# Choice of experts split into single operations, logits in four blocks, the last logits kept on chip, w1 loaded early, five idle TensorE products

## What is computed

```python
def _L0_conv_ref(x, ...):          # attention over all tokens of an image, after a group norm
    h = group_norm(x, gn_scale, gn_bias, 16)
    q, k, v = nin(h, wq, bq), nin(h, wk, bk), nin(h, wv, bv)
    w = softmax(q @ k^T * C ** -0.5)
    return x + nin(w @ v, wo, bo)

t = t + _L1_attn_ref(_ln_t(t), Wq, Wk, Wv)      # causal attention, after a LayerNorm

def _L1_ffn_ref(x, gate_w, gate_b, weight1, weight2):     # x = _ln_t(t); 32 experts
    logits = einsum('bsd,ed->bse', x, gate_w) + gate_b
    probs = softmax(logits, axis=1)                        # over the tokens
    topv, topi = top 8 tokens of each expert
    pooled = einsum('bked,bke->bed', x[topi], topv)
    out = gelu(pooled @ weight1) @ weight2                 # with bias rows
    outputs[topi] += out * topv
t = t + outputs
```

## Time and profile before

| | us |
|---|---|
| median of 3 runs | 900.59 (899.41 to 900.7) |
| the profiled execution | 901.2 |
| its span in the profile | 899.4 |
| busy: PE / DVE / ACT / POOL | 803.9 / 566.2 / 506.4 / 371.0 |

### The profile page before, as it was taken

How to read it: one execution, slowest core, us unless ns; L and a number is a source line. 1 busy time by engine, 2 the same in 40 slices (tenths; PEclk the granted TensorE clock), 3 DMA queues, 4 the chain that set the end, 5 groups by cost and what they waited for, 6 DMA issues and landing times. The chain is left out here.

```text
span 899.4 us, 14859 instructions
## 1 busy us (share of the span) xinstructions
PE 803.9 (89%) x4406; PEld 473.2 (53%) x4406; DVE 566.2 (63%) x1493; ACT 506.4 (56%) x1096; POOL 371.0 (41%) x288
## 2 busy tenths in 40 slices
PE   4586999999999999999999999999999997755286
PEld 2253556565656565656565656565656553433155
DVE  3427476767676767676767676767777755451224
ACT  3153567676767666666676666666666663533120
POOL 3062536363636364545454545455454543100000
PEclk9997899999999999999999999999999998958558
DMA  1000000000000000000000000000000020010798
GB/s 46 0 1 12 1 13 25 18 24 19 24 19 24 19 24 18 24 18 24 18 24 18 24 18 24 18 24 18 24 18 24 7 71 30 1 31 1 147 239 230
DMA packets 62997, 30.54 MB, mean 34 GB/s; under 512 B 35279, under 2 KB 60271, under 8 KB 62959
## 3 DMA queue, kind: packets, MB, share of 16 engines
q1 hardware_dynamic: 62959, 30.05, 13.5%
HBM read 15.23 MB, written 10.49 MB: 29 GB/s over the span
## 5 line engine op out<-in xcount | busy, mean ns | idle before, releaser
L1025 DVE TENSOR_REDUCE neg_max<-maxima_in 128x1 f32<-128x1024 f32 (+7 forms) x256 | 252.0, 984 | 94.3 <-PE maxima_in L654 90.8
L862 ACT ACTIVATE probs<-scores 128x512 f32<-128x512 f32 (+3 forms) x464 | 233.0, 541 | 118.0 <-PE scores L681 106.4
L934 POOL TENSOR_TENSOR prob_sum<-prob_sum,probs 128x1024 f32<-128x1024 f32 x96 | 228.2, 2377 | 8.8 <-ACT probs L862 0.6
L654 PE MATMUL maxima_in<-keys,queries 128*128 128x512 f32 (+3 forms) x496 | 172.6, 422 | 17.3 <-DVE neg_max L1025 14.4
L681 PE MATMUL scores<-queries,keys 128*128 128x512 f32 (+3 forms) x464 | 173.0, 373 | 0.0
L654 PEld LDWEIGHTS maxima_in<-keys,queries 128*128 128x128 f32 x496 | 85.9, 200 | 89.9 <-DVE neg_max L1025 57.4
L696 PE MATMUL values_out<-probs,x_sb 128*64 128x512 f32 x512 | 129.4, 612 | 0.0
L908 POOL TENSOR_TENSOR ln<-ln_mv,eps_ln 128x8 f32<-128x8 f32 x32 | 6.5, 203 | 297.8 <-DVE ln_mv L1059 297.8
L679 PE MATMUL scores<-queries_lo,keys_hi 65*128 65x512 f32 x256 | 109.8, 429 | 2.2 <-DMA queries_lo<-max_rows 1.2
L681 PEld LDWEIGHTS scores<-queries,keys 128*128 128x128 f32 x464 | 90.5, 195 | 8.2
L696 PE MATMUL values_out<-probs,normed 128*64 128x128 f32 (+3 forms) x480 | 84.5, 441 | 0.1
(11 more groups left out here) (169 smaller groups left out, 1102.7 us busy)
## 6 DMA issues: line engine op xcount, KB each, us to landing
x_sb<-in_x SPq DMA_DIRECT2D x16, 256.0 KB, 2.9
u_all<-u_sb SPq DMA_DIRECT2D x16, 256.0 KB, 2.5
t_scratch<-t SPq DMA_DIRECT2D x16, 256.0 KB, 2.9
total<-t_scratch SPq DMA_DIRECT2D x16, 256.0 KB, 4.8
w_sb<-in_w SPq DMA_DIRECT2D x1, 2080.0 KB
logits_scratch<-logits SPq DMA_DIRECT2D x32, 64.0 KB, 2.1
lg<-logits_scratch SPq DMA_DIRECT2D x4, 512.0 KB, 3.7
out<-total SPq DMA_DIRECT2D x16, 128.0 KB, 2.2
```

The lines of the kernel that those rows point to most:

```text
L654: mm = pe.matmul(maxima_in[:, lo:lo + w * P], weights, keys[s][q][:, h * HALF:h * HALF + w * P], start=not diagonal, stop=True, skip_group ...
L862: nc.scalar.activation(of(probs[:, t % NP, :]), shape(scores[:, bank_of(s, u), 0:w]), ACT.Exp, scale=SCALE).then_inc(exp_done, 1)
L934: nc.gpsimd.tensor_tensor(prob_sum[:, :], before, probs[:, t % NP, :], ALU.add).then_inc(rows_added, 1)
L1025: V.tensor_reduce(neg_max[s][:, at:at + 1], maxima_in[:, HALF - widths[0] * P:HALF + widths[1] * P], AX.X, ALU.max, negate=True).then_inc( ...
```

## The change

- e.top becomes three steps, e.max, e.rep and e.ne. A table EXPERT_SLOTS says which step runs in which slot, for each engine apart, and the groups have a semaphore each (expert_step0 to 3). In turn 15 VectorE has one step in a slot, and TensorE's transposes start in slot 5.
- mlg makes the logits of an image in two products of 256 columns into 128 partitions of fin_ps, lg is one copy of 128 x 256, and sl has four stores of 32 partitions, where it had two of 64. gate_b_sb has 128 rows, filled by four loads.
- The last image: its products go to partitions 96 to 127 of two banks, from the halves of ut apart (64 rows each), and ScalarE writes them with the bias straight into the tile lg. SyncE loads the other three images of that group right after the last store of u.
- w1 lies over the keys and queries of the first attention. ScalarE issues its load in turn 15 after the last exponential of the first attention.
- expert_part: three products of 512 columns that nobody reads ahead of the last choice, one ahead of the turn by image, one ahead of the sums.
- In ScalarE's list lg comes ahead of its slot 0, and l1n ahead of its slots 5 and 6. Neither changes anything while the slots are empty.

```diff
+EXPERT_SLOTS = {
+    "dve": {0: [("e.max", 0)], 1: [("e.rep", 0)], 2: [("e.ne", 0)], 3: [("e.gate", 0)], 4: [("e.max", 1)], 5: [("e.rep", 1)],
...
-    if n == B:
-        return [(EXPERT_STEPS[k % 7], k // 7) for k in (2 * c, 2 * c + 1) if k < 14]
-    if n == B + 1 and c < 7:
-        return [(EXPERT_STEPS[c], 2)]
-    return []
+    return EXPERT_SLOTS[engine].get(c + NT * (n - B), [])
...
-                   (gate_b_sb[0:E, :], g["gate_b"]), (gate_b_sb[E:2 * E, :], g["gate_b"])]
+                   *[(gate_b_sb[r * E:(r + 1) * E, :], g["gate_b"]) for r in range(P // E)]]
...
+                if n.trip is None and n.first == B - 1:
+                    load_logits(NG - 1, BG - 1)
+            elif name == "sl" and (n.trip is not None or n.first < B - 1):
...
-                dst = image_of(logits_dram, at).rearrange("e (j a t) -> a e j t", a=2, t=P)
-                for a in range(2):
-                    sp.dma_start(dst[a], logits[a * E:(a + 1) * E, :].rearrange("e (j t) -> e j t", t=P)).then_inc(
-                        logits_stored, 16)
+                dst = image_of(logits_dram, at).rearrange("e (h j a t) -> h a e j t", h=2, a=2, t=P)
+                for h, a in itertools.product(range(2), range(2)):
+                    r = (2 * h + a) * E
+                    sp.dma_start(dst[h, a], logits[r:r + E, :].rearrange("e (j t) -> e j t", t=P)).then_inc(logits_stored, 16)
...
+            elif name == "mlg" and n.trip is None and n.first == B - 1:
+
+                pe.wait_ge(proj_step, done("proj_step", "yb", n, "lo"))
+                for a, bank in enumerate((fin_ps, proj_ps)):
+                    r = slice(a * C, (a + 1) * C)
+                    mm = pe.matmul(bank[P - E:P, :], gate_bd[r, a * E:(a + 1) * E], ut[r, :], start=True, stop=True)
+                mm.then_inc(fin_step, 1)
...
-                pe.matmul(fin_ps[0:2 * E, :], gate_bd[:, :], ut[:, :], start=True, stop=True).then_inc(fin_step, 1)
+                for h in range(2):
+                    mm = pe.matmul(fin_ps[h * 2 * E:(h + 1) * 2 * E, 0:HALF // 2], gate_bd[:, :],
+                                   ut[:, h * HALF // 2:(h + 1) * HALF // 2], start=True, stop=True)
+                mm.then_inc(fin_step, 1)
...
+            elif name == "lg" and n.trip is None and n.first == B - 1:
+                act.wait_ge(fin_step, done("fin_step", "mlg", n, "mm"))
+                act.wait_ge(g["expert_step"][NG - 3], done(f"expert_step{NG - 3}", "e.ne", NG - 3, "chosen"))
+                for a, bank in enumerate((fin_ps, proj_ps)):
+                    ins = nc.scalar.activation(
+                        g["lg"][P - E:P, (NG - 1) % 2, :].rearrange("p (j a t) -> p a j t", a=2, t=P)[:, a, :, :],
+                        bank[P - E:P, :].rearrange("p (j t) -> p j t", t=P), ACT.Identity, bias=gate_b_sb[P - E:P, :], scale=1.0)
+                ins.then_inc(fin_step, 1)
...
+            if s == 1 and u == len(UNITS[1]) - 1 and n.trip is None and n.first == B - 1:
+
+                nc.scalar.dma_start(g["w1_sb"][:, :, :], g["w1"].rearrange("e d h -> d e h")).then_inc(g["w1_loaded"], 16)
...
-        k = LAST_GROUP
-        sp.dma_start(g["lg"][:, k % 2, :], logits_dram[k * BG:(k + 1) * BG].rearrange("b e s -> (b e) s")).then_inc(
-            g["logits_loaded"][k], 16)
-        sp.dma_start(w1_sb[:, :, :], g["w1"].rearrange("e d h -> d e h")).then_inc(w1_loaded, 16)
...
+        def keep_clock(times, bank):
+
+            for _ in range(times):
+                pe.matmul(hidden_ps[:, bank, :], ident_f[:, :], g["u_all"][:, 0, 0:HALF], start=True, stop=True)
+
+        keep_clock(3, BANKS - 1)
...
         mm.then_inc(out_ready, 1)
+        keep_clock(1, 0)
         pe.wait_ge(out_biased, 1)
...
         mm.then_inc(image_turned, 1)
+        keep_clock(1, 0)
         pe.wait_ge(image_copied, 2)
```

More of the change, by code:

```diff
@@ L237, in choose_on_vector @@
 def choose_on_vector(nc, g, name, k):
-    V, step, lg, rest, top, stat, gates = (nc.vector, *(g[n] for n in ("expert_step", "lg", "rest", "top", "stat", "gates")))
+    V, lg, rest, top, stat, gates = (nc.vector, *(g[n] for n in ("lg", "rest", "top", "stat", "gates")))
+    step = g["expert_step"][k]
     def after(step_name):
-        before = done("expert_step", name, k, step_name, back=1)
+        before = done(f"expert_step{k}", name, k, step_name, back=1)
         if before > 0:
             V.wait_ge(step, before)
-    if name == "e.top":
-        after("max")
+    if name == "e.max":
         V.wait_ge(g["logits_loaded"][k], 16)
@@ L251, in choose_on_vector @@
         V.tensor_scalar(stat[:, k, 0:1], top[:, k, 0:1], -1.0, None, ALU.mult).then_inc(step, 1)
+    elif name == "e.rep":
+        if k > 0:
+            V.wait_ge(g["expert_step"][k - 1], done(f"expert_step{k - 1}", "e.gate", k - 1, "gates"))
+        after("rest")
         V.match_replace(rest[:, :], top[:, k, :], lg[:, k % 2, :], NEG_HUGE).then_inc(step, 1)
+    elif name == "e.ne":
         after("chosen")
@@ L263, in choose_on_scalar @@
 def choose_on_scalar(nc, g, name, k, turn, pool_ps):
-    step, gates, gates_t, pool_sb, pooled = (g[n] for n in ("expert_step", "gates", "gates_t", "pool_sb", "pooled"))
+    gates, gates_t, pool_sb, pooled = (g[n] for n in ("gates", "gates_t", "pool_sb", "pooled"))
+    step = g["expert_step"][k]
     if name == "e.exp":
-        nc.scalar.wait_ge(step, done("expert_step", "e.top", k, "neg"))
+        nc.scalar.wait_ge(step, done(f"expert_step{k}", "e.max", k, "neg"))
         nc.scalar.activation(gates[:, k, :], g["lg"][:, k % 2, :], ACT.Exp, bias=g["stat"][:, k, 0:1], scale=1.0,
@@ L284, in choose_on_tensor @@
 def choose_on_tensor(nc, g, name, k, turn, pool_ps):
-    pe, step, gates, gates_t, u_all, pool_sb, ident_f = (nc.tensor, *(
-        g[n] for n in ("expert_step", "gates", "gates_t", "u_all", "pool_sb", "ident_f")))
+    pe, gates, gates_t, u_all, pool_sb, ident_f = (nc.tensor, *(
+        g[n] for n in ("gates", "gates_t", "u_all", "pool_sb", "ident_f")))
+    step = g["expert_step"][k]
     if name not in ("e.ta", "e.tb", "e.pool", "e.turn"):
         return
-    pe.wait_ge(step, done("expert_step", name, k, EXPERT_STEP_COUNT[name][0]) - 1)
+    if name == "e.ta" and k > 0:
+        pe.wait_ge(g["expert_step"][k - 1], done(f"expert_step{k - 1}", "e.turn", k - 1, "copy"))
+    pe.wait_ge(step, done(f"expert_step{k}", name, k, EXPERT_STEP_COUNT[name][0]) - 1)
     if name == "e.pool":
@@ L635, in piece @@
                 name, k = in_bank.pop("step")
-                pe.wait_ge(g["expert_step"], done("expert_step", name, k, "copy"))
+                pe.wait_ge(g["expert_step"][k], done(f"expert_step{k}", name, k, "copy"))
             block_c = c if s == 1 else query_block(c)
@@ L840, in run @@
                 if exists(n + (-1)):
-                    act.wait_ge(logits_stored, each(n + (-1), 32))
-                nc.scalar.activation(logits[:, :], fin_ps[0:2 * E, :], ACT.Identity, bias=gate_b_sb[:, :],
+                    act.wait_ge(logits_stored, each(n + (-1), 64))
+                nc.scalar.activation(logits[:, :], fin_ps[:, 0:HALF // 2], ACT.Identity, bias=gate_b_sb[:, :],
                                      scale=1.0).then_inc(fin_step, 1)
@@ L1172, in _ @@
         pe.wait_ge(w1_loaded, 16)
-        pe.wait_ge(expert_step, done("expert_step", "e.turn", LAST_GROUP, "copy"))
+        pe.wait_ge(expert_step[LAST_GROUP], done(f"expert_step{LAST_GROUP}", "e.turn", LAST_GROUP, "copy"))
         for quad in range(QUADS):
```

54 lines of the change are left out of this document (33 added, 21 removed), and 6 rows, old and new, of the table ORDER.

## The result

The changed kernel took 877.33 us in the median of 4 runs (876.66 to 878.42), the kernel before 900.64 in the same session (899.41 to 902.65): ratio 0.9742, 95% interval 0.9721 to 0.9763, so 23.3 us less. I had forecast 892.6 and a range that began at 879. The sign was right, the size was a third of the truth. The profiled execution took 876.66 us, its span is 874.9 (before: 899.4), so 24.5 us of span are to be found.

A forecast was written before the change was run, and what follows sets the result against it. TensorE's work plus every hole was taken to bound a loop turn, half-idle chains the last 160 us. Terms of +0.8 +7.5 +0.6 -10.2 +1.8 -5.8 -0.85 -1.0 -0.8 took 900.6 to 892.6 us; range 879 to 902.5.

The forecast's parts named there:

- What bounds the kernel: Loop turn: TensorE's work plus every hole sets its cost; nearest hole at the row copy, slack 0.29 us.
- Part 1: Start: gate_b_sb loaded to four blocks instead of two, with nothing hiding the two more loads: +0.8 us.
- Part 2: Logits in four blocks: four stores delay the row copy and the score; +7.5 us in the loop, +0.6 outside.
- four take twice that: Logits stores in the loop: two took 1.61 us to the row copy's issue, four would take double.
- Rival B: Loop logits: narrower stores cheap or product change worth its half microsecond, no hole; 878 us, up to 886; chance 0.16.
- Part 3: Turn 15: no choice steps ahead of attention's first score, so the cast comes 10.2 us earlier (bounds 6 and 13).
- rival D: Turn 15: w1's load occupies the DMA engines, row copy lands behind it; 903.4 us; chance 0.12 with other mishaps.
- Part 4: Turn 16: later row copy, plus a pooling and a turn behind the score: +1.8 us (0 to +3).
- Part 5: Last logits: without the trip through DRAM, products side by side, the maximum comes earlier: -5.8 us (-4 to -6).
- Part 6: First hidden product: w1 loaded ahead, so it waits only for the pooled inputs: -0.85 us.
- Part 7: Five idle products in the tail raise TensorE's clock: -1.0 us for the three, -0.8 for the two single ones.

The follow-up runs named there:

- the first of the two attempts above: Changed kernel with w1's load late and two idle products inside the last choice, plus eight more idle products around the last logits and choice: 874.37 us.
- the two kernels of the idle products' section: Kernel before with only the five idle products added: 900.22 us; changed kernel with the last logits again stored to DRAM and loaded back: 890.63 us.

## Why the prediction was wrong, step by step

**What bounds the kernel**: right. TensorE's row and its holes set a turn, and the slack at the row copy was as small as read in the earlier trace rows: with eight stores a copy issued 2.15 us later behind the logits product made a wait of 1.95 us. There the score came 2.04 us after the issue of the copy that it waited for, so the 2.07 of the changed kernel leave it next to no slack.

**Part 1** (+0.8): the wait for the bias is 6.6 us instead of 6.1, the row copy of image 0 0.6 later. The four loads took 1.71 us, 0.43 each.

**Part 2** (+8.1): the step that failed by sign. The terms for product and copy held: the product takes 0.65 for 1.07, the bias copy 0.47 for 0.68. The term "four take twice that" did not: from the first store to the issue of the copy it is 1.95 us (519.41 to 521.36), against 1.61 for two and 3.2 in the forecast, and each store takes 0.46 instead of 0.75. I had both ends on the table, 0.39 for a bias load of 32 x 1 and 0.75 for a logits store of 32 x 512, and took the upper one because it was a store to the same tensor, as if its price did not depend on its columns. The new store has as many partitions as both and half the bytes of the old one, and it came out next to the lower end. So the copy went out earlier behind the product and not 1 us later, and there was no hole: -5.3 by the stores of turn 14 with the start's 0.6 in it, and -4.3 (2.9 to 5.8) for the whole part measured alone, in place of +8.1. Rival B, to which I gave 0.16, is what happened here. That its 878 is also the time measured is luck: its other terms missed by 5.3 us one way (part 3) and 6.9 the other (parts 6 and 7).

**Part 3** (-10.2): the removal of choice steps was read rightly, and the score, forecast for 752.2, at 751.81 only agrees by accident. Counted from the logits stores of turn 15 it is 10.1 us behind them (741.67), before it was 10.9 (749.50). The logits stores themselves came 2.5 us earlier than the turns before explain, with no choice step ahead of them, and the way from the score to the cast is 16.5 us instead of 18.1. So the cast at 768.27 is 10.2 us earlier than in the earlier trace rows, the very number of the forecast, but 5.3 of it is inherited from the turns before and 4.9 is this part; the other 5.3 went to rival D. With w1 late my sum of parts 3 and 4 (8.4) is met in size, 8.8, but some 2 of it are not from the new places, which are worth about 7.2.
Rival D was right in its mechanism and too dear in its price: I had the copy land behind all of w1's packets, near 763, and it landed 8 us after its issue with w1's load under way. I halved its chance on the word of the Trainium skill (DMA: Bandwidth & Descriptors, Issuing engines are not separate DMA queues). By that page of the Trainium skill transfers of different engines interleave on the same DMA engines. The trace agrees that the copy did not wait for the whole load; it took 8.06 us to the score instead of 2.07 all the same.

**Part 4** (+1.8): the score of turn 16 starts 1.83 us after the issue of its copy, before it was 2.55, and the pooling behind it takes 1.94 us at half clock, as said. From the cast of the keys to the last store of u it is 55.94 us against 54.17: +1.8.

**Part 5** (-5.8): 6.1 by the traces. The two halves of the product ran side by side: both start at 826.10 and take 1.06. The Trainium skill (TensorEngine Tiling (Array Packing), Key Properties), which I had drawn on for this price, says that different tiles can load weights and multiply in parallel, and this trace agrees.

**Part 6** (-0.85): right; nothing releases the hidden products but the pooled inputs.

**Part 7** (-1.8): the second large miss, behind part 2. I had the mechanism, the clock, and bounds that reached -8, and then counted on TensorE's idle half to bring the clock down again. It did not fall: up at 833.5, it stayed until 850.6 through the gaps of 0.3 to 0.9 us in the choice. All of the earlier trace rows from the first transpose on went at twice the speed or nearly: 2.3 us in the choice (0.85 of it w1's), 4.9 from the hidden products to the end of w2's, 3.2 in the sums, less 0.9 for the single products in their gaps. The term should have been -8.7. (The +0.7 for the second single product was a slip too: 1.97 less a gap of 1.00 is 0.97.) That it also hangs on part 5 I had not seen at all: I added the two, and alone the idle products are worth nothing.

So the forecast missed by 15.3 us (16.6 in the spans): 14.2 in parts 1 and 2, 6.9 in parts 6 and 7, 0.3 in part 5 and 0.5 at the end, less 5.3 that rival D took from part 3.

What stays open is what makes the clock fall within a stretch that looks busy in the rows. With nearly the same work it fell at 850.6, 837.2, 841.5 or 844 in neighbouring kernels. Runs of one kernel differ by 6 to 8 us, and the clock goes with it: in the first of the two attempts above the runs of 871.29 and 871.38 us have a mean granted clock of 0.970 and 0.968, those of 877.37 and 877.51 us 0.959 and 0.960. With two fillers in the gaps four runs lay within 1.6 us; with more of them they lay 6.2 apart again. I can't say from these traces when a fall must come.

## What to carry to other kernels

The issue of a DMA on SyncE cost 0.43 to 0.50 us here up to 32 x 256 elements and 0.75 for 32 x 512: cutting each store in two raised the price of all of an image's stores from 1.49 to 1.84 us, and cutting them once more from 1.84 to 3.99. So where no row has the shape, lay the sum once with the nearest row above and once with the nearest below, and don't choose between them by the name of the tensor. Then count what stands behind it, since a row copy that came 2 us late cost 2.5 us in every turn. Idle products pay only where real work follows them closely; so judge them together with whatever closes the gap behind them, and give them a price by laying both clocks against every row up to the next long wait. And when a part of a change removes the steps ahead of a wait, look at what another part starts in just that moment: here moving one load by 7 us was worth more than the new places had been.

## What I had not expected of the hardware

- Of 64 hidden products at 0.50 and at 1.00 of the clock: 7.05 and 3.66 us; of 128 w2 products with 16 columns: 7.02 and 3.91. Even such short products take nearly twice as long.
- After the hidden products began at half clock, it took the clock 10.8 us to rise in the kernel before (856.9 to 867.7), and 25.5 in the changed one without idle products (843.6 to 869.1), for nearly the same instructions. In the two kernels of the idle products' section that send the last logits through DRAM it was 11 to 12 us.
- A small DMA (the row copy, 8 rows of 128 numbers) issued by SyncE 3.3 us after ScalarE's 2 MB load needed 8.06 us to the score that waits for it; with the load behind it TensorE didn't wait for it at all, 3.17 us after its issue.
- Issue of a DMA on SyncE: 0.43 (32 x 1 from DRAM), 0.46 (32 x 256 in two pieces), 0.50 (32 x 128), 0.75 (32 x 512 in four pieces).
